# The mixer's row sums of squares: eight accumulating one-column matmuls in place of GpSimd's additions and one matmul

## What is computed

```python
y = ys.transpose(1, 0, 2, 3) + D_skip[None, None, :, None] * x
y = y.reshape(b, l, D_INNER)
y = y * jax.nn.silu(gate)
var = jnp.mean(y * y, axis=-1, keepdims=True)
y = y * jax.lax.rsqrt(var + EPS) * norm_w
return jnp.einsum('bld,do->blo', y, W_out)
```

## Time and profile before

| | |
|---|---|
| time, median of 3 executions | 1049.43 us (1049.27 to 1051.59) |
| the profiled execution: its own time | 1053.63 us |
| the profiled execution: span from first to last instruction | 1051.9 us |
| mean granted TensorE clock over the span | 0.982 of 2.4 GHz |
| busy over the span | PE 95%, PEld 79%, DVE 77%, ACT 61%, POOL 32% |
| the mixer | from the start to about 427 us |
| matmul and weight-load records | 7360 each |

### The profile page before, as it was taken

One profiled execution on the slowest core, in us unless ns is written; L12 is line 12 of the kernel. 1 busy time (PEld: TensorE's weight loads), 2 busy tenths in 40 slices (PEclk: granted clock), 3 DMA queues, 4 the chain that ended last, 5 costly groups with the idle time before them and its releaser, 6 DMA issues.

```text
span 1051.9 us, 19604 instructions
## 1 busy us (share of the span) xinstructions
PE 1000.2 (95%) x7360; PEld 833.6 (79%) x7360; DVE 813.6 (77%) x1431; ACT 646.1 (61%) x1337; POOL 340.8 (32%) x465
## 2 busy tenths in 40 slices
PE   4979999999999997899999999999999999999997
PEld 4879898989989986789899999976545875875873
DVE  5789999999999998748666866886867766766763
ACT  6876777868677684565665566567231761761760
POOL 2014142341524134343435334323431331331331
PEclk9789999999999998999999999999999999999999
DMA  7530404132140336410011011223511101101001
GB/s 230 179 111 8 152 25 138 49 110 102 56 148 11 134 112 222 163 50 11 31 44 41 1 41 41 71 81 120 176 45 63 59 2 59 63 1 50 31 2 60
DMA packets 44702, 81.36 MB, mean 77 GB/s; under 512 B 7360, under 2 KB 17600, under 8 KB 42560
## 3 DMA queue, kind: packets, MB, share of 16 engines
q1 hardware_dynamic: 44608, 80.11, 22.3%
HBM read 67.24 MB, written 12.85 MB: 76 GB/s over the span
## 4 chain that ended last, share of the span: by engine, by line
PE 71%; DVE 13%; ACT 6%; DMA 3%; issue 3%; POOL 3%; SPq 0%; POOLq 0%; DVEq 0%; ACTq 0%
PE banks L815 26%; PE banks L2186 13%; PE banks L2254 11%; PE banks L1541 8%; PE banks L2177 3%; PE banks L1509 3%; PE banks L931 3%; PE banks L923 1%; DVE c_cv L1364 1%; PE banks L879 1%; PE banks L908 1%; DMA d_wd_codes<-in_down_w 1%; DVE c_gx L1388 1%; DVE c_mu L1379 1%; DVE c_xb L1343 1%
## 5 line engine op out<-in xcount | busy, mean ns | idle before, releaser
L2254 PE MATMUL banks<-d_wd,d_hh 128*128 128x512 f16 x256 | 97.0, 379 | 0.0
L2254 PE MATMUL banks<-d_wd,d_hl 128*128 128x512 f16 x256 | 97.0, 379 | 0.0
L651 DVE SCALAR_TENSOR_TENSOR a_xs<-a_xpre,a_cvec,a_xs 128x256 f32<-128x256 f32 x192 | 92.1, 544 | 0.0
L1837 POOL TENSOR_TENSOR d_hl<-d_h32s,d_hh 128x512 f16<-128x512 f32 x48 | 55.6, 1159 | 102.3 <-ACT d_hh L1932 102.3
L815 PE MATMUL banks<-a_xth,a_wxh 128*128 128x256 f32 x256 | 75.4, 295 | 3.3 <-ACT a_xs L454 3.3
L341 POOL TENSOR_TENSOR a_sg<-a_sg 128x512 f32<-128x512 f32 x16 | 20.9, 1305 | 170.6 <-ACT a_sg L446 170.6
L676 DVE TENSOR_TENSOR_SCAN a_L<-a_L,a_ident 128x512 f32<-128x512 f32 x64 | 74.7, 1209 | 0.5
L815 PE MATMUL banks<-a_xth,a_wgh 128*128 128x256 f32 x256 | 75.0, 293 | 0.0
L815 PE MATMUL banks<-a_xtl,a_wxh 128*128 128x256 f32 x256 | 73.2, 286 | 0.0
L815 PE MATMUL banks<-a_xth,a_wxl 128*128 128x256 f32 x256 | 73.1, 285 | 0.0
L815 PE MATMUL banks<-a_xth,a_wgl 128*128 128x256 f32 x256 | 72.8, 285 | 0.0
(11 more groups left out here) (347 smaller groups left out, 3253.7 us busy)
## 6 DMA issues: line engine op xcount, KB each, us to landing
a_L<-decays SPq DMA_DIRECT2D x16, 1024.0 KB, 4.8
a_xf<-in_x_turned SPq DMA_DIRECT2D x16, 256.0 KB, 3.9
a_xr<-in_x SPq DMA_DIRECT2D x16, 256.0 KB, 2.7
tokens<-a_xr SPq DMA_DIRECT2D x16, 256.0 KB, 2.1
c_xb<-tokens SPq DMA_DIRECT2D x16, 256.0 KB, 3.1
d_xin<-tokens SPq DMA_DIRECT2D x16, 256.0 KB, 3.8
d_r<-tokens SPq DMA_DIRECT2D x16, 256.0 KB, 2.7
d_wd_codes<-in_down_w SPq DMA_DIRECT2D x4, 1024.0 KB, 10.2
```

The costliest lines, as they stand in the source:

```text
L651: ins = dve.scalar_tensor_tensor(out=out, in0=xpre[:, m, k:k + T], scalar=cvec[:, m, k:k + 1], in1=out, op0=ALU.mult, op1=ALU.add)
L1837: pool.tensor_tensor(hl[:, m, :], (h32s[:, m % 4, :] if i else h32[:, m % 2, :]), hh[:, m, :], ALU.subtract).then_inc(s_hl, 1)
L2254: ins = pe.matmul(ps_o[:, c % 2, :], h[:, m, cols(c)], wd[:, m, :], start=(m == 0 and h is hh), stop=(m == M - 1 and h is hl), skip_group_ ...
```

## The change

The three additions on POOL and their semaphore go. PE's `sum_sq` waits for ACT's squares (`s_sq`) instead of POOL's sum, and adds the eight blocks itself: eight fp32 matmuls, each with one block of squares as weights and the column of ones as the moving operand, accumulate in the same column of PSUM; the last raises `s_sp`.

```diff
@@ gpsimd
-        def tree(n):
-            j = n % C
-            sq = sg[:, :, cols(j)]
-            pool.wait_ge(s_sq, n + 1)
-            order(pool.tensor_tensor(sq[:, 0:4], sq[:, 0:4], sq[:, 4:8], ALU.add))
-            order(pool.tensor_tensor(sq[:, 0:2], sq[:, 0:2], sq[:, 2:4], ALU.add))
-            pool.tensor_tensor(sq[:, 0], sq[:, 0], sq[:, 1], ALU.add).then_inc(s_tree, 1)
...
             if s:
-                tree(C * s - 2)
                 scale(C * s - 2)
-                tree(C * s - 1)
                 norm(C * s - 2)
...
         following_stage["bound"](0)
-        tree(C * NS - 2)
         following_stage["bounded_norm"](0)
-        tree(C * NS - 1)
         scale(C * NS - 2)
@@ tensor
         def sum_sq(n):
             j = n % C
-            pe.wait_ge(s_tree, n + 1)
+            pe.wait_ge(s_sq, n + 1)
             wait(pe, s_rv, n)
             pe.wait_ge(s_ya, R * C * (n // C + 1))
-            pe.matmul(ps_q[:, j:j + 1], sg[:, 0, cols(j)], ones, start=True, stop=True).then_inc(s_sp, 1)
+            for m in range(M):
+                last = pe.matmul(ps_q[:, j:j + 1], sg[:, m, cols(j)], ones, start=m == 0, stop=m == M - 1)
+            last.then_inc(s_sp, 1)
```

More of the change, by code:

```diff
@@ L197, in mamba2 @@
     s_stp, s_stm, s_su, s_in, s_yp = (sem(n) for n in ("stp", "stm", "su", "in", "yp"))
-    s_ya, s_yg, s_yh, s_sq, s_yl, s_tree, s_sp, s_rv, s_rs = (
-        sem(n) for n in ("ya", "yg", "yh", "sq", "yl", "tree", "ssqp", "rv", "rs"))
+    s_ya, s_yg, s_yh, s_sq, s_yl, s_sp, s_rv, s_rs = (
+        sem(n) for n in ("ya", "yg", "yh", "sq", "yl", "ssqp", "rv", "rs"))
     s_op, s_res, s_var, s_std, s_done = (sem(n) for n in ("op", "res", "var", "std", "done"))
```

## The result

| | before | after |
|---|---|---|
| median of 4 executions (us) | 1050.06 (1049.27 to 1051.59) | 1073.46 (1070.99 to 1074.68) |
| ratio, 95% interval | | 1.0216 (1.0203 to 1.0229) |
| the profiled execution: own time, span (us) | 1053.63, 1051.9 | 1070.99, 1069.3 |
| first sum starts (us) | 82.0 | 79.1 |
| from one stage's first sum to the next, mean of six (us) | 47.15 | 50.29 |

The changed kernel is slower by 2.16%, 22.7 us by the ratio; 21.1 was forecast, and 1073.46 lies in the range of 1065.5 to 1074.0, near its upper end.

A forecast was written before the change was run, and what follows sets the result against it. PE was taken to bound stages 1 to 7; +21.6 us for their sums and -0.5 at the mixer's end gave +21.1, from 1049.43 to 1070.5 us. The range was 1065.5 to 1074.0 us.

The forecast's parts named there:

- PE is the bound in stages 1 to 7: From 80 to 385 us PE is busy all 305 us at clock 1.00; added PE work costs its whole price.
- 0.11 us a pass: PE's sums: 14 more passes each, paced by weight loads, 1.54 us a sum, +21.6 us over 14 sums.
- rival A: PE's sums: short matmuls cost little, 0.03 us for each added pass, slower by about 5, 1054.8 us; chance 0.05.
- POOL's additions are worth nothing in the stages: Stages 1 to 7: removing 44 us of POOL work gains nothing and only adds to DVE's idle time.
- The moved wait and DVE's slack cost nothing: PE's wait for ACT's squares costs nothing; DVE's longer wait for the sum is hidden, its 1.2 us of slack stays.
- The end, -0.5 us: Mixer's end: two sums add 1.54 us each, DVE loses 1.9 us of disturbance; -0.5 taken, bounds -1.9 to +3.1.
- L1343's 0.82 us: DVE's update of `c_xb`: 1.76 us with POOL's L341 beside it, read as 0.82 alone.
- the 0.94 us of delay: DVE's delay beside POOL's L341, less than L341's whole 1.29 us, explained by DVE starting 0.08 later.
- B: Loads exposed at 188 ns each, 1085.7 us, or the clock falls in the mixer, costing tens of us; together chance 0.08.
- C: DVE is the true bound, PE has 1.54 us free at each sum; 8.5 us gained, 1041 us; chance 0.02.
- D: Whole kernel: no change, needing PE free and DVE of no use, or the two cancelling; chance 0.01.

The follow-up runs named there:

- the half-loaded kernel: Changed kernel with blocks 1 to 7 loading 64 of their 128 columns, so half the tokens' sums leave features out; 1065.24 us, ratio 1.0143.
- the one without accumulation: Changed kernel with each of the eight matmuls writing its own PSUM column, so the mean counts block 0 alone; 1069.58 us, one execution.
- the two traces of the changed kernel: The changed kernel, unaltered, measured again beside the follow-up kernels: 1071.06 us, ratio 1.0196; its first measurement was 1073.46 us, ratio 1.0216.
- the kernel with the change at the end alone: Kernel before, with the new sum for chunks 14 and 15 only, their POOL additions left out; 1050.47 us, ratio 1.0002.
- with cheap passes: Changed kernel with squares and ones in bfloat16, one pass for a block instead of two; 1050.61 us, ratio 1.0002.
- the one with four blocks: Kernel before, with POOL adding only blocks 4 to 7 onto 0 to 3 and PE summing four blocks; 1059.97 us, ratio 1.0082.

## Why the prediction was right

- *PE is the bound in stages 1 to 7.* Right, and it carries everything: PE 326 of 326 us busy at clock 1.00, the six stages together longer by 18.85 us, which is 12 x 1.57.
- *0.11 us a pass.* Right: 0.112. A sum costs 1.785 and 1.740 us at its two places where it cost 0.224 and 0.176, so 1.56 more, forecast 1.54; 21.9 us over 14 sums, forecast 21.6. That the load sets this pace was an inference from the transposes; the half-loaded kernel shows it, and the one without accumulation excludes the nearest other cause. This holds for fp32 only: in bfloat16 the prediction's rival A has its 0.03 us a pass, and the trace shows 0.025. The 25 ns floor that the Trainium skill (TensorE: Matmul & The Clock Gate, Back-to-back issue gap) names agrees with it. The Trainium skill's formula in the section LDWEIGHTS of the same page, by which 128 columns take 107 ns, names no type; it agrees with the 112 ns of fp32 and not with the bfloat16 loads.
- *POOL's additions are worth nothing in the stages.* Right within 0.1 us a stage. DVE did get faster, by 22.5 us of busy time, and spent all of it waiting for PE. The size of what was removed was put too low, 44 us by the median durations; the three additions come to 52.7 us over the trace of before, since some were much longer than the median (1604 and 1328 ns), and that cost the forecast nothing.
- *The moved wait and DVE's slack cost nothing.* Right: no wait of PE, and the slack behind the second sum is 1.3 us against 1.2. The idle time of DVE there was underestimated ("more than 2", measured 5.63), without consequence.
- *The end, -0.5 us.* -0.24 and -0.8 in the two traces of the changed kernel, -0.2 in the kernel with the change at the end alone. The forecast lies among them, and that it is so close is in part luck, since single traces differ here by as much as its size. The reason given, PE too late to let DVE's gain through, is what the trace shows (0.74 us late), and with cheap passes the gain came whole, -2.0, where the bound had -1.9. Two readings behind it were wrong without consequence. L1343's 0.82 us was not "alone", as said above. And the 0.94 us of delay is not explained by DVE starting 0.08 us behind L341, which would leave 1.21 of the 1.29. Nor does L1352, with one input, fall outside the page that the prediction cites: the Trainium skill (SBUF — State Buffer, Who interferes with whom) also lists `tensor_scalar` among the instructions that can take the shared ports in a two-port mode. No run here shows in which mode L1352 ran.
- *Rivals* (the prediction's letters). A falls for fp32, and so does B: the starts are not 0.19 apart and the clock in stages 1 to 7 is not under 1.00. C and D fall by the time.

## What to carry to other kernels

In a stretch where the chain of waits never leaves one engine, moving work to it from an idle engine costs its whole price, and freeing the idle engine gives nothing back. Where the engine does wait, as PE at the mixer's end, it gave up to 2.0 us back. The price of the one-column matmuls here was that of their weight loads: count loads by the distance between starts, 0.11 us for 128 fp32 columns, and two for each fp32 matmul. If such a reduction has to go to TensorE, give it 16-bit operands where the squares may be rounded to them: the eight blocks then cost 0.30 us in place of 1.79.

## What was not expected of the hardware

A bfloat16 load of 128 columns followed by a one-column matmul goes at 0.025 us from start to start, where its own record lasts 0.096; fp32 goes at 0.112 with a record of 0.192. From the records alone a factor of two would have been expected; it is 4.5.

Executions differ before the first sum, in a part of the program that the change hardly touches. The stretch from 0 to 79 us, with the columns of the earlier trace rows, in the kernel before, the changed one and the one with four blocks:

```profile
0.00:79.00 79.00, 57.84 (x438) 53.72 (x439) 58.41 (x92) 58.93 (x121) 10.89 (x33) 0.87 0.52 173
```

```profile
0.00:79.00 79.00, 57.61 (x450) 52.60 (x451) 61.16 (x101) 59.64 (x123) 7.43 (x30) 0.94 0.52 174
```

```profile
0.00:79.00 79.00, 58.96 (x444) 54.35 (x445) 60.69 (x98) 59.93 (x123) 8.76 (x31) 0.89 0.53 173
```

The granted clock is 0.87, 0.94 and 0.89 and the first sum starts at 82.0, 79.1 and 80.5 us: the lower the clock was on average, the later it came. Over all ten traces 0.94 goes with 78.5 to 80.1 us, 0.91 with 80.0, 0.89 with 80.5 and 81.2, and 0.87 with 82.0. In this stretch PE waits for transfers and the splitting of weights; nothing of the change is in it but the first additions on POOL. That the clock is the cause was not tested. The 3.5 us between them are as large as the spread of the first times, 2.3 us before and 3.7 after, and a reason to compare stages by starts within a trace before comparing spans.
